# Projection stages of a graph kernel: Newton roots on VectorE, all normalising on ScalarE, a ring of seven, and map-row gathers moved to the first aggregation

## What is computed

```python
h = jnp.maximum(_layernorm(x, axis=-1), 0.0)
x = x + L0(h)     # three rounds of attention over edges, each h' = h + sigmoid(conv(h))
h = jnp.maximum(_layernorm(x, axis=-1), 0.0)
x = x + L1(h)     # 100 relation types built from 4 basis matrices, sum by target node, relu
h = jnp.maximum(_layernorm(x, axis=-1), 0.0)
x = x + L2(h)     # attention with 8 heads of 16 channels
h = jnp.maximum(_layernorm(x, axis=-1), 0.0)
x = x + L3(h)     # messages |h[dst] - h[src]|, sum by target node, two linear maps

def conv(x):      # one head; L2 is the same with eight
    h = x @ W
    e = leaky_relu((h @ a_src)[src] + (h @ a_dst)[dst])
    w = exp(e - segment_max(e, dst)[dst])
    return segment_sum((w / segment_sum(w, dst)[dst])[:, None] * h[src], dst) + b
```

## Time and profile before

| what | us |
|---|---|
| median of 3 runs | 4129.71 (4114.74 to 4135.91) |
| the profiled execution | 4123.5, of which 4121.8 are its span |
| keys | 22 to 263 |
| local_chain | 274 to 1308 |
| project 0 | 1311.8 to 1510.7 (198.9) |
| rows_found | 1514.8 to 1518.5 |
| aggregate 0 | 1539.1 to 1684.7 (145.6) |
| project 1, project 2 | 198.2, 195.8 |
| aggregate 1, aggregate 2 | 142.3, 161 |
| relate | 2439 to 2816 |
| project 4 | 2823.7 to 3028.3 (204.6) |
| edge_messages, edge_outputs | 679, 170 |

### The profile page before, as it was taken

How to read it: one execution, slowest core, us unless ns; L and a number is a source line. 1 busy time by engine, 2 the same in 40 slices (tenths; PEclk the granted TensorE clock), 3 DMA queues, 4 the chain that set the end, 5 groups by cost and what they waited for, 6 DMA issues and landing times. The chain is left out here.

```text
span 4121.8 us, 57885 instructions
## 1 busy us (share of the span) xinstructions
PE 2421.4 (59%) x13649; PEld 1953.8 (47%) x13649; DVE 2277.9 (55%) x7669; ACT 1509.5 (37%) x3239; POOL 2159.3 (52%) x1921
## 2 busy tenths in 40 slices
PE   1136899999996647466465637775636444433433
PEld 1123676667676546466454634454626332322222
DVE  3145999899896655223423448885674333333223
ACT  0006999999994641121122013222420022222100
POOL 3628675557645850350064236555820278877755
PEclk9998999999998875686588559887865576666655
DMA  2140132333212537441654363323312533333243
GB/s 61 31 167 24 47 103 88 90 96 106 88 51 67 143 100 228 140 123 47 177 152 109 112 187 95 95 86 87 111 29 81 151 74 72 73 70 72 53 137 114
DMA packets 570788, 405.84 MB, mean 98 GB/s; under 512 B 51549, under 2 KB 497702, under 8 KB 570146
## 3 DMA queue, kind: packets, MB, share of 16 engines
q1 hardware_dynamic: 513650, 356.21, 28.7%
q0 software_dynamic: 56000, 46.29, 6.0%
q10 hardware_dynamic: 880, 0.41, 0.0%
HBM read 270.38 MB, written 158.24 MB: 104 GB/s over the span
## 5 line engine op out<-in xcount | busy, mean ns | idle before, releaser
L1147 POOL DMA_INDIRECT p_ends_state<-t_d,p_ends_ix x300 | 316.0, 1053 | 568.0 <-issue 279.7
L806 POOL TENSOR_TENSOR a_rs<-a_ve,w_neg_half 128x16 f32<-128x16 f32 x113 | 330.4, 2924 | 243.1 <-DVE a_ve L742 211.8
L1367 PE MATMUL p_pm<-w_aug,p_ht 128*128 128x130 f32 (+1 forms) x1600 | 327.9, 326 | 165.1 <-ACT p_ht L1321 107.4
L832 ACT ACTIVATE a_nr<-a_xb,a_nm,a_rs 128x128 f32<-128x128 f32 x882 | 370.4, 488 | 26.1 <-POOL a_nm L808 26.1
L1972 POOL DMA_INDIRECT e_a<-t_d,e_ix x200 | 209.4, 1047 | 298.1 <-DMA e_a<-t_s 235.9
L1367 PEld LDWEIGHTS p_pm<-w_aug,p_ht 128*128 128x128 f32 x1600 | 272.0, 231 | 187.0 <-issue 135.1
L894 PE MATMUL a_ps<-w_ident,a_nr 128*128 128x128 f32 x1568 | 247.7, 282 | 126.7 <-ACT a_ht L840 47.0
L902 PE MATMUL a_ps<-a_ht,w_aug 128*128 128x512 f32 x588 | 316.8, 624 | 2.4 <-DVE a_ht L709 2.4
L894 PEld LDWEIGHTS a_ps<-w_ident,a_nr 128*128 128x128 f32 x1568 | 181.9, 144 | 275.8 <-issue 243.1
L1697 PE MATMUL c_ps<-layer_src,c_sel 128*128 (+1 forms) x800 | 192.0, 419 | 192.3 <-DMA c_sel<-t_sel 107.8
L709 DVE TENSOR_TENSOR a_ht<-a_ps,a_ht 128x512 f32<-128x512 f32 x294 | 201.9, 688 | 135.2 <-ACT a_ps L847 117.8
(11 more groups left out here) (362 smaller groups left out, 6724.9 us busy)
## 6 DMA issues: line engine op xcount, KB each, us to landing
t_s<-p_ends_state SPq DMA_DIRECT2D x100, 256.0 KB
c_sel<-t_sel SPq DMA_DIRECT2D x100, 256.0 KB
c_a<-t_d SPq DMA_DIRECT2D x100, 256.0 KB
t_d<-c_a SPq DMA_DIRECT2D x100, 256.0 KB
a_xa<-in_x SPq DMA_DIRECT2D x98, 256.0 KB
out<-a_xb SPq DMA_DIRECT2D x98, 256.0 KB, 2.0
p_ends_state<-t_s SPq DMA_DIRECT2D x75, 256.0 KB
p_ends_state<-t_d SPq DMA_DIRECT2D x75, 256.0 KB
```

Of the source, the lines that this page charges most:

```text
L806: nc.gpsimd.tensor_tensor(RS[:, z, :], VE[:, z, :], w["neg_half"][:, None, 0:J].to_broadcast([P, LNS, J]), ALU.pow).then_inc(s_rstd.sem, 1)
L832: last = nc.scalar.activation(NR[k][:, T.at(NORM[k], 2), cols(j)], normed_rows(T, k)[:, cols(j)], ACT.Identity, bias=NM[:, T.at(1, SHORT), ...
L1147: eng.indirect_dma_start(out=self.A[:, g, SRC, j, :], out_offset=None, in_=self.t[self.dst_table], in_offset=bass.IndirectOffsetOnAxis(ap= ...
L1367: last = nc.tensor.matmul(PM[side][:, j, 0:CW], HT[:, g, side, j * C:(j + 1) * C], rhs, start=side == SRC, stop=True)
```

## The change

- A class `Moments` takes the place of `Norms` in `project`. The inverse root is made on DVE by three Newton steps from an integer first guess: 13 operations on 128x8, woven one by one between the moments (`turn`) of the next block. POOL no longer takes part.
- ACT normalises both sides, with the rectifier fused in "first". DVE takes both sides out of PSUM with the bias added (`hold`); the bias matmuls L1366 and ACT's copy L1327 are gone.
- The index of each gather is read straight from `k["map_ix"]`; DVE's copies of indices (L1139, L1253) and words (L1258) are gone. No engine of `project` has a loop any more.
- The ring of state blocks has 7 slots instead of 5. SP issues store(b), then load(b + 6). A load waits for the store of its slot and for the target product of its slot.
- The 100 map-row gathers are no longer in `project` 0. `aggregate` 0 issues them on POOL in a row, straight into `f["found"]`, now integers; `rows_found` comes after it, with three more casts.

The core of the diff:

```diff
-        "found": sb("found", [P, TX, WORDS]),
+        "found": sb("found", [P, T, WORDS], I32),
...
-            done(v.tensor_copy(k["map_ix"][:, :], f["found"][:, 0:T, 0]))
-
-            done(v.tensor_copy(OWNER[:, :], f["found"][:, 0:T, 1]))
+            done(v.tensor_copy(k["map_ix"][:, :], f["found"][:, :, 0]))
+
+            done(v.tensor_copy(OWNER[:, :], f["found"][:, :, 1]))
             for j in range(1, J):
-                done(v.tensor_tensor(OWNER[:, :], OWNER[:, :], f["found"][:, 0:T, 1 + j], ALU.min))
+                done(v.tensor_copy(TMP[:, :], f["found"][:, :, 1 + j]))
+                done(v.tensor_tensor(OWNER[:, :], OWNER[:, :], TMP[:, :], ALU.min))
...
+class Moments:
+    STEPS = 12
+    def newton(self, eng, b, step):
+        v, g = self.nc.vector, b % self.ring
+        ve, half, square, y = self.var_eps[:, g, :], self.half[:, g, :], self.square[:, g, :], self.rstd[:, g, :]
+        if step == 0:
+            eng.wait_ge(self.s_moments, b + 1)
+            v.tensor_scalar(ve, self.moments[:, g, :, 1], LN_EPS, None, ALU.add).then_inc(self.s_newton, 1)
+            return
+        eng.wait_ge(self.s_newton, b * (self.STEPS - 1) + step)
+        if step == 1:
+            v.tensor_scalar(half, ve, -0.5, None, ALU.mult)
+            v.tensor_scalar(y.bitcast(I32), ve.bitcast(I32), -0.5, 1597463007.0, ALU.mult, ALU.add).then_inc(self.s_newton, 1)
+        elif step == self.STEPS - 1:
+            v.scalar_tensor_tensor(self.shift[:, g, :], self.moments[:, g, :, 0], -1.0, y, ALU.mult, ALU.mult).then_inc(self.s_shift, 1)
+        elif step % 3 == 2:
+            v.tensor_tensor(square, y, y, ALU.mult).then_inc(self.s_newton, 1)
+        elif step % 3 == 0:
+            v.tensor_tensor(square, square, half, ALU.mult).then_inc(self.s_newton, 1)
+        else:
+            v.scalar_tensor_tensor(y, square, 1.5, y, ALU.add, ALU.mult).then_inc(self.s_newton, 1)
+    def turn(self, eng, rows, b, last):
+        v = self.nc.vector
+        step = 0
+        for n in range(self.n):
+            if b <= last:
+                ins_ = v.bn_stats(self.stats[:, b % self.ring, n, :], rows(n))
+                if n == self.n - 1:
+                    ins_.then_inc(self.s_stats, 1)
+            if b and step < self.STEPS:
+                self.newton(eng, b - 1, step)
+                step += 1
+        if b <= last:
+            eng.wait_ge(self.s_stats, b + 1)
+        for n in range(self.n):
+            if b <= last:
+                ins_ = v.bn_aggr(self.moments[:, b % self.ring, n, :], self.stats[:, b % self.ring, n, :])
+                if n == self.n - 1:
+                    ins_.then_inc(self.s_moments, 1)
+            if n % 2 and b and step < self.STEPS:
+                self.newton(eng, b - 1, step)
+                step += 1
+        assert not b or step == self.STEPS
...
+    first, normed = kind == "first", kind == "normed"
+    sigmoid, norm, overlay = not normed, kind != "plain", not first
+    RING, SHORT = 7, 3
...
+            def load(b):
+                g = b % RING
+                if b >= RING:
+                    eng.wait_ge(s_out[g], (uses(b) - 1) * OUTS)
+                    eng.wait_ge(s_mm[DST], b - RING + 1)
+                for side in (SRC, DST):
+                    eng.dma_start(A[:, g, side, :, :], block_rows(t[tables[side]], b)).then_inc(s_load[g], 16)
+            def load_x(b):
+                if b >= SHORT:
+                    eng.wait_ge(s_plus, b - SHORT + 1)
+                eng.dma_start(XS[:, b % SHORT, :, :], block_rows(t["xs"], b)).then_inc(s_xs[b % SHORT], 16)
+            def store(b):
+                g = b % RING
+                if first:
+                    eng.wait_ge(s_normed[DST], b + 1)
                     eng.dma_start(block_rows(t["d0"], b), A[:, g, DST, :, :]).then_inc(s_out[g], 16)
-                wait(eng, s_next, b + 1)
-                carry_waits(eng, w)
+                eng.wait_ge(s_next, b + 1)
                 eng.dma_start(block_rows(t[f"s{r + 1}"], b), A[:, g, SRC, :, :]).then_inc(s_out[g], 16)
 
-            stream(eng, (load, 0), (store, 4))
-            for g in range(GE):
-                eng.wait_ge(s_out[g], OUTS * ROUNDS_E)
-
-        @block.gpsimd
-        def _(eng):
-            def map_rows(b, g):
-                wait(eng, ends.s_index, b + 1)
-
-                wait(eng, s_found, b - GE + 1)
-                carry_waits(eng, w)
-                for j in range(J):
-                    eng.indirect_dma_start(out=ROWS[:, g, j, :], out_offset=None, in_=t["maps"].rearrange("(n a) o -> n (a o)", a=WORDS),
-                                           in_offset=bass.IndirectOffsetOnAxis(ap=ends.IX[:, g, j:j + 1], axis=0),
-                                           bounds_check=NODES - 1, oob_is_err=False).then_inc(s_map[g], 16)
-
-            steps = [(map_rows, 2)] if kind == "first" else []
-            if ends.overlay:
-                steps.append((lambda b, g: ends.gather(eng, b, g), 0))
-            if norm:
-                steps.append((lambda b, g: nb.invert(eng, b, g), 1))
-            stream(eng, *steps)
+            for b in range(RING):
+                load(b)
+                if plus_x and b < SHORT:
+                    load_x(b)
+            for b in range(BLOCKS):
+                store(b)
+                if b and b - 1 + RING < BLOCKS:
+                    load(b - 1 + RING)
+                if plus_x and b + SHORT < BLOCKS:
+                    load_x(b + SHORT)
+            for g in range(RING):
+                eng.wait_ge(s_out[g], OUTS * len(range(g, BLOCKS, RING)))
+        if overlay:
+            @block.gpsimd
+            def _(eng):
+                for b in range(BLOCKS):
+                    g = b % RING
+                    eng.wait_ge(s_load[g], uses(b) * 32)
+                    for j in range(J):
+                        eng.indirect_dma_start(out=A[:, g, SRC, j, :], out_offset=None, in_=t[f"d{r}"],
+                                               in_offset=bass.IndirectOffsetOnAxis(ap=k["map_ix"][:, b * J + j:b * J + j + 1], axis=0),
+                                               bounds_check=EP - 1, oob_is_err=False).then_inc(s_over[g], 16)
...
+            def hold(b):
+                for side in (SRC, DST):
+                    eng.wait_ge(s_mm[side], b + 1)
+                    v.tensor_tensor(held(("src", "dst")[side], b)[:, :, 0:CW], PM[side][:, :, 0:CW], wide, ALU.add).then_inc(s_keep[side], 1)
+
+            def residual(b):
+                g, grow = b % RING, UP[:, b % SHORT, :, :] if sigmoid else held("src", b)[:, :, 0:C]
+                if sigmoid:
+                    eng.wait_ge(s_sig, b + 1)
+                else:
+                    eng.wait_ge(s_keep[SRC], b + 1)
+                if plus_x:
+                    eng.wait_ge(s_xs[b % SHORT], (b // SHORT + 1) * 16)
+                    v.tensor_tensor(grow, grow, XS[:, b % SHORT, :, :], ALU.add).then_inc(s_plus, 1)
+                    eng.wait_ge(s_plus, b + 1)
+                there(eng, b, SRC)
+                v.tensor_tensor(A[:, g, SRC, :, :], A[:, g, SRC, :, :], grow, ALU.add).then_inc(s_next, 1)
+
+            holds, residuals = (3, 4) if norm else (0, 1)
+            for n in range(BLOCKS + residuals):
+                if norm and n <= BLOCKS:
+                    if n < BLOCKS:
+                        there(eng, n)
+                    mo.turn(eng, lambda m: A[:, n % RING, m // J, m % J, :], n, BLOCKS - 1)
+                if 0 <= n - residuals:
+                    residual(n - residuals)
+                if 0 <= n - holds < BLOCKS:
+                    hold(n - holds)
...
+            def apply(b):
+                g, m = b % RING, b % SHORT
+                eng.wait_ge(mo.s_shift, b + 1)
+                if normed and b >= SHORT:
+                    eng.wait_ge(s_mm[DST], b - SHORT + 1)
                 for side in (SRC, DST):
-                    wait(eng, nb.s_normed[side], (b + 1) * J)
-                    nc.scalar.activation(A[:, g, side, :, :], A[:, g, side, :, :], ACT.Relu).then_inc(s_relu, 1)
-
-            def copy(b, g):
+                    for j in range(J):
+                        n = side * J + j
+                        rows = A[:, g, side, j, :]
+                        last = nc.scalar.activation(NR[:, m, side, j, :] if normed else rows, rows, ACT.Identity if normed else ACT.Relu,
+                                                    bias=mo.shift[:, m, n:n + 1], scale=mo.rstd[:, m, n:n + 1])
+                    last.then_inc(s_normed[side], 1)
...
+        if first:
+            s_found = sem("found")
+
+            @block.gpsimd
+            def _(eng):
+                for n in range(T):
+                    eng.indirect_dma_start(out=f["found"][:, n, :], out_offset=None, in_=t["maps"].rearrange("(n a) o -> n (a o)", a=WORDS),
+                                           in_offset=bass.IndirectOffsetOnAxis(ap=f["map_at"][:, n:n + 1], axis=0),
```

(8 more changed lines are left out.)

## The result

The changed kernel takes 4190.1 us (median of 4 runs, 4184.96 to 4198.55) beside 4122.2 for the kernel before: ratio 1.016, interval 1.013 to 1.020, so slower by 1.3 to 2.0%. The forecast of 4129, no difference to speak of, was wrong; the time is near the 4204 of rival E. The profiled execution has a span of 4196.8 against 4121.8. On two other chips where `keys` takes as long as here the ratio was 1.017 both times. On a chip where `keys` takes 169 us instead of 241, a kind that the experiments met by chance, it is 0.986.

A forecast was written before the change was run, and what follows sets the result against it. POOL was taken to bound project 0, and late PE signals during unbroken gather trains to hold other stages; project 0 -48, rows_found +1, aggregate 0 +73, projects 1, 2 and 4 -15, -12, 0 gave -1: 4129 us, range 4000 to 4195.

The forecast's parts named there:

- rival E: Aggregate 0 and projections: late signals cost more than forecast, seven slots run dry; +75, 4204 us; chance 0.18.
- Project 0: Roots and gathers leave POOL, DVE then sets the cycle at 5.3 a block: 151 us, -48, range -48 to 0.
- The low price of the small operations: Project 0, DVE: thirteen small operations a block, woven between independent moments, at 0.08 each, 1.04 us.
- the 5.3 of the sum: Project 0, DVE per block: moments 2.33, three adds 2.0, small operations 1.04; sum 5.3 to 5.4 us.
- a gain from unrolling itself: Projections: disappearing loops priced at nothing; the trace has no room for such a gain in project 0.
- project 4: POOL loses 50 us of roots, but these break the trains; takes the form of project 1: 0, range -25 to +15.
- signals on time: Projections without late signals: POOL alone bounds projects 1 and 2, -52 and -50; project 4 -40.
- Aggregate 0: 100 gathers in an unbroken train delay PE's signals in the opening part: +73, range 0 to +82.
- signals that arrive 18.5 us late: Read from keys: while POOL issues gathers unbroken, PE's signals reach other engines up to about 18.5 us late.
- Projects 1 and 2: Seven slots mean fewer ring rounds and pauses, but longer trains: -15 and -12, range -25 to +5 each.
- B: Aggregate 0 and projections: no late signals where it matters; -189, 3941 us; chance 0.11.
- The sum: Whole kernel: -48 + 1 + 73 - 15 - 12 + 0 = -1, 4129 us against the median.

The follow-up runs named there:

- e4_ring9: The changed kernel with 9 ring slots instead of 7 in project 4 alone: 3839.8 us, 0.973 of the kernel before.
- e18_after: The changed kernel itself once more, on a chip without the effect: 3885.6 us beside 3939.8, ratio 0.986.
- e12_train: The kernel before with 100 additional map-row gathers in a row on POOL in aggregate 0, into an unread buffer: 4190.2 us beside 4104.3.
- e5: The changed kernel itself, again, on a chip with keys at 240: 4193.3 us beside 4122.7, ratio 1.017.
- e6: The changed kernel with 9 ring slots in project 4, on a chip with keys at 240: 4169.4 us, ratio 1.012.
- e11: The changed kernel itself, on a chip with the effect: 4174.2 us beside 4104.3, ratio 1.017.
- e16_pow: The kernel before with 78 inverse roots in a row on POOL in aggregate 0, no DMA, chip with keys at 239: 4120.9 us beside 4126.3.
- e17_broken: The changed kernel, nine slots in project 4, gather trains broken in keys, projections and aggregate 0, chip with the effect: 3978.8 us beside 4126.3, ratio 0.964.
- e13_pow: The kernel before with 78 inverse roots in a row on POOL in aggregate 0, no DMA, chip without the effect: 3932.1 us.
- e15_broken: The changed kernel, nine slots in project 4, gather trains broken in keys, projections and aggregate 0, chip without the effect: 3937.5 us beside 3939.1, ratio 1.000.

## Why the prediction was wrong, step by step

- **Project 0** was right, -47.8 against -48, with some luck in the parts. The low price of the small operations was right, and DVE's turn is 4.9 us where it doesn't wait, less than the 5.3 of the sum. But about every second turn is 6.0 to 6.8, with over 1 us of waits for PE's products, which the sum didn't have. The mean of the turns came to 5.3 and start and drain to 23 where 18 were put down: 151.1 was worked out as 151. The total leaves no room for a gain from unrolling itself; no run tests that alone.
- **The largest step that failed: project 4**, +39.2 against 0. The forecast priced it by trains and had it as project 1 with the normalising ahead. It named that a load waits for the store of its slot, and did not follow that wait round. SP issues load b + 6 behind store b, and store b follows DVE's residual, four turns behind the moments. So a load runs two blocks ahead of the moments that need it, whatever the seven slots suggest. Two blocks then cost load, gathers and a turn, 17.9 us in the trace or 8.9 a block. e4_ring9 removes it, 223 to 168, on a chip without the effect. Against the kernel before, seven slots are +19 there, so about half of the +39 here is the ring alone; the other half comes only with the effect, in the first train of 28 and the pause of 27 behind it (6.4 in e18_after). Nine slots are -36 there, near the -40 that the forecast had for signals on time, and still +18 here.
- **Aggregate 0** had the right cause and place and the wrong mechanism, and so the wrong size: +105.8 against +73 (0 to +82). The forecast read the keys rows as signals that arrive 18.5 us late, and counted four of them. The rows after show that instructions themselves are held up: little of the opening part goes on between 20 us after the train's start and its end, and 54 of PE's 200 records, 27 of the 100 products, are then still to be done. The loss is the held stretch, 1502 to 1621, 119 us, less what still gets through in it: 57 records, which take 12 us at full pace. That makes 107, and PE's last product is 153.6 into the stage and was 46.6 before, +107. e12_train gives +100 for the train alone. (A map row is five integers, 20 bytes and not 160; nothing hangs on it.)
- **Projects 1 and 2**, -11.5 and -6.2 against -15 and -12: no more than a size, and within what these stages vary by with unchanged code. The first trains are of 28 gathers as forecast, with breaks of 11 to 13. What the ring and the lags give without the effect is seen on the other kind of chip: project 1 is bound by POOL and equal before and after (147), and project 2 gains 21.
- **The rivals.** E had the sign and nearly the sum, 4204 against 4190, by luck: it had +15 each for projects 1 and 2, which got shorter, +10 for project 4, which got 39 longer, and +82 for aggregate 0, which got 106 longer. B, "no late signals", is what happens on the other kind of chip, with 0.986 instead of the 0.95 it was given. There the kernel before is free of the effect too and takes 177 to 187 us less, so projects 1 and 2 gain 0 and 21 instead of 52 and 50, and project 4 takes 19 longer by its ring instead of gaining 40. That the price of a stage in the one profile depends on the chip was not among the rivals, and could not be seen in one trace.
- **The sum** balanced a gain of 48 against a loss of 73 and took the projections as nearly free; with the measured terms it would have been +80. Of the 81 us between the two sums, 39 are project 4, 33 aggregate 0 and 9 projects 1 and 2.

## What to carry to other kernels

Follow a ring's slot once round, through the order of the queue that issues loads and stores and the lag of the last reader: slots minus lag minus one is how far the loads run ahead, and moving a reader later takes that away even when slots are added. Where indirect DMAs are moved into an unbroken row on one engine, look in the traces at hand for the longest such row and at what every other engine does during it, instruction by instruction; breaking the row up gains where the others are held (0.964 against 1.012 with nine slots and unbroken rows) and costs where they are not (1.000 against 0.973), so measure both on the chips that the kernel is to run on. Repeat a profile on another chip before a stage's idle time is taken for a property of the kernel.

## What the runs showed of the hardware

- On the chips of the first measurement, of e5 and e6, of e11 and e12, and of e16 and e17, a long row of indirect DMAs at 1.30 us each held up the other engines. In aggregate 0 it did so from 21 us (changed kernel) and 28 us (e12_train) after its start to 5 or 6 us after its end, in the end with the records of DVE and SP alternating at 0.70 us; until then all went at full pace. In keys (kernel before) it shows as silences of 13 to 18 us of all engines but POOL, the first 19 us after the start. At the head of project 1, before the change, one silence of 8.5 us begins 14 us after the start of a row of 16, and e13_pow has none there. 131 us of other POOL work did nothing of the kind (e16_pow).
- On the chips of the other runs there was none of it; keys has a single silence there, of 11 us (e13_pow, e18_after). The kernel before takes 3939 to 3946 there and 4104 to 4126 here; keys alone is 169 to 173 against 239 to 242, project 1 147 against 194 to 206.
- A break of about 2 us after eight indirect DMAs (10.4 us) is enough to avoid nearly all of it in keys, project 1, project 2 and aggregate 0: e17_broken is there within 5 us of e15_broken. Project 4 stays 12 us longer.
- Why the chips differ stays open, as does what is being used up. Three chips were without the effect, and three or four with it (the first measurement may have been on one that was met again). One was met twice, without it both times, and none was met in both kinds, so that it goes with the chip and not with the session is likely but rests on that. Each of these executions was one whose instructions were recorded, and the held-up streams move record by record, at 3.1 to 3.7 records of all engines a us, in keys (3.5) as in aggregate 0 (3.7, and 3.1 in e12_train). That is what a limit on the recording would look like, and is no proof of one; whether an execution that is not recorded shows the effect was not tried. If it doesn't, the 1.016 and the gain of the broken rows belong to the recorded executions alone.
